# Decoder layer with selective scan, attention and top-2 experts: raw rows scattered, keys and values on ScalarE, routing scratch in PSUM

## The reference

```python
def mixer(x):                       # x: layernorm of the input
    h = layernorm(x) * ln_g + ln_b
    x_h, res = split(h @ W_in.T)    # 256 + 256 channels
    x_h = silu(causal_conv(x_h, 4 taps))
    dt, B, C = split(x_h @ W_x.T)   # 64, 16, 16
    dt = softplus(dt @ W_dt.T + b_dt)
    # scan over 256 positions, state 256 x 16:
    #   h = exp(dt * A) * h + dt * B * x_h ;  y = sum(h * C)
    y = (scan + x_h * D_param) * silu(res)
    return x + alpha * (y @ W_out.T)
x = x + mixer(layernorm(x))
x = x + cross_attention(layernorm(x), ctx, 16 heads, 64 keys, mask)
g = layernorm(x)
p = softmax(g @ Wg + bg)            # 8 experts
top 2 of p, weights softmax(p1, p2)
x = x + sum over the two of weight * (relu(g @ W1[e] + b1[e]) @ W2[e] + b2[e])
```

## Time and profile before

| what | value |
|---|---|
| median of 3 runs | 1040.76 us (1035.5 to 1041.91) |
| the profiled execution's own time | 1042.74 us |
| its span in the profile | 1040.9 us |
| busy: TensorE, VectorE, GpSimd, ScalarE | 787.0, 744.2, 704.4, 488.9 us |
| granted TensorE clock, mean | 0.865 of full |
| moved by DMA | 143.51 MB, 138 GB/s on average |
| longest scan-phase group on VectorE | scan L1332, 128 times, 292.6 us |

### The profile page before, as it was taken

The page is one execution under the profiler, slowest core; times in us unless marked ns, Lnnn a source line. Parts: engine busy times, 40 slices in busy tenths (PEclk is TensorE's granted clock), DMA queues, the critical chain, the costliest instruction groups (busy, mean ns, idle before and its releaser), DMA issues. The chain is left out here.

```text
span 1040.9 us, 12598 instructions
## 1 busy us (share of the span) xinstructions
PE 787.0 (76%) x3871; PEld 498.4 (48%) x3871; DVE 744.2 (71%) x1060; ACT 488.9 (47%) x1086; POOL 704.4 (68%) x501
## 2 busy tenths in 40 slices
PE   5667677797778778867877886774768998799592
PEld 1233343363344345334524542452446688798592
DVE  3279987989996897899789889958952625233172
ACT  3557456557475545746564674434213334232130
POOL 0159987978699779878977996787661445554252
PEclk9888788998899679878976997776688999999797
DMA  2324382282264228225522642385016446867872
GB/s 67 126 101 147 125 246 95 93 214 84 91 179 139 84 96 225 90 91 149 167 84 83 190 127 75 121 202 162 1 37 194 132 116 178 255 187 196 270 215 79
DMA packets 111076, 143.51 MB, mean 138 GB/s; under 512 B 18392, under 2 KB 83557, under 8 KB 111008
## 3 DMA queue, kind: packets, MB, share of 16 engines
q1 hardware_dynamic: 106016, 134.26, 43.9%
q0 software_dynamic: 4992, 8.45, 2.5%
HBM read 110.48 MB, written 34.01 MB: 139 GB/s over the span
## 5 line engine op out<-in xcount | busy, mean ns | idle before, releaser
L1185 POOL TENSOR_TENSOR prod<-hst,BC 128x1024 f32<-128x1024 f32 x128 | 303.9, 2374 | 121.6 <-DVE hst L1332 120.3
L1332 DVE TENSOR_TENSOR_SCAN hst<-dA,Rp 128x1024 f32<-128x1024 f32 x128 | 292.6, 2286 | 12.2 <-DVE Rp L1323 0.4
L993 ACT ACTIVATE dA<-dtm,Aneg 128x255 f32<-128x255 f32 x512 | 216.0, 495 | 146.4 <-DVE hst L1332 146.2
L571 PE MATMUL Y<-prod,ident 128*128 128x256 f32 x512 | 167.7, 461 | 65.0 <-POOL prod L1190 58.6
L1266 POOL DMA_INDIRECT y2d<-prod,BC x92 | 90.6, 984 | 136.6 <-DVE prod L1627 114.9
L571 PEld LDWEIGHTS Y<-prod,ident 128*128 128x128 f32 x512 | 108.5, 225 | 140.7 <-POOL prod L1190 93.8
L1190 POOL TENSOR_TENSOR prod<-prod 128x512 f32<-128x512 f32 x128 | 163.6, 1278 | 10.0
L1323 DVE TENSOR_TENSOR Rp<-BC,Rp 128x1024 f32<-128x1024 f32 x128 | 156.5, 1223 | 5.5 <-DMA BC<-bcd 1.5
L571 PE MATMUL Rp<-BC,prod 128*128 128x128 f32 x736 | 92.0, 279 | 8.2 <-DVE prod L1627 8.2
L571 PE MATMUL T<-Kbd,qT 64*128 64x512 f32 x128 | 62.5, 862 | 45.9 <-DVE mx L1376 45.9
L571 PEld LDWEIGHTS Rp<-BC,prod 128*128 128x128 f32 x736 | 90.5, 195 | 13.3 <-issue 10.8
(11 more groups left out here) (222 smaller groups left out, 1255.7 us busy)
## 6 DMA issues: line engine op xcount, KB each, us to landing
BC<-bcd SPq DMA_DIRECT2D x64, 1024.0 KB, 5.4
BC<-in_L_ffn_W SPq DMA_DIRECT2D x92, 256.0 KB
xsd<-blank SPq DMA_DIRECT2D x18, 1032.0 KB, 13.8
BC<-xsd SPq DMA_DIRECT2D x46, 129.0 KB
soft<-in_L_ffn_b SPq DMA_DIRECT2D x46, 64.0 KB
xin<-in_x SPq DMA_DIRECT2D x8, 256.0 KB, 4.1
x2d<-x2o SPq DMA_DIRECT2D x8, 256.0 KB
E<-x2d SPq DMA_DIRECT2D x1, 2048.0 KB
```

Source lines behind the costliest of these rows:

```text
L571: return pe.matmul(o, l, r_, start=start, stop=stop, **kw)
L993: m = A(dA[:, k % RING, i, 1:SEQ], dtm[:, r % 2, d, b * SEQ + 1:(b + 1) * SEQ], ACT.Exp, scale=Aneg[:, d, c * NC + i:c * NC + i + 1])
L1185: TT(prod[:, k % RING, :, :], hst[:, k % RING, :, :], BC[:, (k // 2) % BCR, 1, :, :], ALU.mult).then_inc(s_pd, 1)
L1332: v.tensor_tensor_scan(hst[:, k % RING].rearrange("p n s -> p (n s)"), dA[:, k % RING].rearrange("p n s -> p (n s)"), U.rearrange("p n s - ...
```

## The change

- The rows that are scattered are the raw ones: `x2o` itself gets 132 words a row, with the negated mean, the reciprocal spread, the token's index and its first expert behind the 128 channels. `rows_out` and `xs` go. The rows are normalised when a group is loaded: VectorE's new `tile_norm(j+2)` (two operations of 128 columns, and two of two elements for the index `back`) stands behind `tile_relu(j)`, and TensorE's `tile_in` waits for it.
- ScalarE copies keys and values (`copy_kv`) and makes `Kbd` in two halves of eight small copies with a scale (`key_blocks`). The contexts are loaded by one DMA of 512 KB and turned in round 0.
- The router's scaled logits are made by GpSimd with opposite sign (`scaled_logits`), VectorE takes their minimum (`least`), ScalarE makes four exponentials with their sums; no division follows in the round (one at the end, `softmax_gaps`). The picks and places pass through PSUM (`Picked`, `Placed`); the step's input product at steps 11 and 13 waits for that scratch. The counting matmuls read both choices, 10 matmuls instead of 5.
- Other slots: `mixer_out`, `logits`, `att_out` on VectorE at step 5 instead of 4; scores and maxima at 10 to 13; turned maxima at 14; `conv` half 1 at 6; turned scores behind the norm's matmuls; spreads at 6; keys and values stay at 6 with the centring after them.
- Scatters: two behind step 13, three behind 14 and 15 each.
- The residual comes in four loads of 512 KB at groups 21, 24, 27 and 30; the results' six loads stand one behind each of six groups' loads.

The diff, cut to what matters:

```diff
@@
-ROW = D + 1
+NM, RS, ID, E0 = D, D + 1, D + 2, D + 3
+ROW = D + 4
...
+        Picked = [t[:, 0:2 * NTT].rearrange("p (c t) -> p c t", c=2) for t in (scratch, sqt)]
...
             for j in range(PARTS[1].group, GROUPS):
                 load_group(j)
-                if j == PARTS[1].group + WR - 1:
+                n = j - PARTS[1].group - WR + 1
+                if n == 0:
                     scattered(PARTS[1].group)
-                    for i in range(early):
-                        load_results(i)
+                if 0 <= n < 2 * early:
+                    load_results(*divmod(n, 2))
...
-                pe.wait_ge(s_xr[j % XR], 16 * (j // XR + 1))
+                pe.wait_ge(s_nm, j + 1)
...
+            def key_blocks(r, half):
+
+                act.wait_ge(Ta.sem, Ta.at("KT", r))
+                if r and half == 0:
+                    act.wait_ge(Tp.sem, Tp.at("st11", r - 1))
+                for h in range(half * HP, (half + 1) * HP):
+                    m = A(Kbd[:, :, h, :], KT[:, :, :], ACT.Copy, scale=blk[:, h:h + 1])
+                m.then_inc(s_kb, 1)
...
-            def rows_out(r):
-
-                if r:
-                    act.wait_ge(s_xs, 16 * 2 * NTT * r)
                 for t in range(NTT):
-                    m = A(xs[:, t, :, 0:D], x2o[:, t, :].unsqueeze(1).to_broadcast([P, 2, D]), ACT.Identity, bias=nmr[:, t:t + 1],
-                          scale=spread[:, t:t + 1])
+                    at = r * NTT + t
+                    m = A(pr[:, t, :], nl[:, t, :], ACT.Exp, bias=lmin[:, t:t + 1], scale=-1.0, accum_out=lsum[:, at:at + 1])
...
-                if tail2 and k < 2 * NTT - 3:
-                    scatter(r - 3, k + 3)
...
+                        for n in ((0, 1), (2, 3, 4), (5, 6, 7))[k - STEPS + 3]:
+                            scatter(r - 2, n)
...
+                if r >= 2 and k in (11, 13):
+                    v.wait_ge(Fv.sem, Fv.at("hot" if k == 11 else "ch", r - 2))
...
+            def tile_norm(j):
+                n = j % XR
+                v.wait_ge(s_xr[n], 16 * (j // XR + 1))
+                if j >= 2:
+                    v.wait_ge(s_tt, j - 1)
+                for i in range(GT):
+                    m = v.tensor_scalar(xl[:, j % 2, i, :], xr[:, n, i, 0:D], xr[:, n, i, NM:NM + 1], xr[:, n, i, RS:RS + 1], ALU.add, ALU.mult)
+                m.then_inc(s_nm, 1)
...
             for j in range(GROUPS):
                 a, b = slots_of(j)
                 tile_relu(j)
+                if j + 2 < GROUPS:
+                    tile_norm(j + 2)
                 if j:
                     tile_out(j - 1)
```

More of the change, by code:

```diff
@@ L211, in decoder @@
         blank = sb("blank", [P, 2, ROW])
[L212 to L213 removed]
+        lg = sb("lg", [P, NTT, EXPERTS])
+        nl = sb("nl", [P, NTT, EXPERTS])
         sqs = sb("sqs", [P, D])
[L215 to L217 removed]
+        lmin = sb("lmin", [P, NTT])
         pr = sb("pr", [P, NTT, EXPERTS])
[L219 removed]
+        lsum = sb("lsum", [P, ROUNDS * NTT])
         top = sb("top", [P, NTT, 8])
@@ L236, in decoder @@
         pasts = xn2[:, 0:PARTS[0].groups * EXPERTS].rearrange("p (g e) -> p g e", e=EXPERTS)
-        expert = sb("expert", [P, PARTS[0].groups])
+        expert = sb("expert", [P, GROUPS])
         start = sb("start", [P, PARTS[0].groups])
@@ L332, in decoder @@
         s_ys = sem("s_ys")
-        s_acc = sem("s_acc")
+        s_acc = [sem(f"s_acc{i}") for i in range(FINAL)]
         s_y = [sem(f"s_y{i}") for i in range(YR)]
@@ L561, in _ @@
             for i in range(early, FINAL):
-                load_results(i)
+                for c in range(2):
+                    load_results(i, c)
             for i in range(early, FINAL):
@@ L1050, in slot @@
                 ln, nxt = ahead(r)
-                prev, tail, tail2 = behind(r)
+                prev, tail = behind(r)
+                if r == 0 and k in (6, 7):
+                    copy_contexts(k - 6)
                 if tail:
@@ L1160, in _ @@
                 if j == PARTS[1].group:
-                    act.wait_ge(Fv.sem, Fv.all(ROUNDS - 1))
-                    A(wt[:, 1, :], gaps[:, :], ACT.Exp).then_inc(s_wt, 1)
+                    act.wait_ge(s_wt, 2)
+                    A(wt[:, 1, :], wt[:, 1, :], ACT.Exp).then_inc(s_wt, 1)
         @block.gpsimd
@@ L1206, in row_ids, with picks, row_slots @@
                     pool.wait_ge(s_xs, 16 * 2 * NTT * r)
-                pool.tensor_copy(xs[:, :, :, D:ROW].bitcast(I32), ids[:, r, :, :].unsqueeze(3)).then_inc(s_id, 1)
+                pool.tensor_copy(x2o[:, :, ID], ids[:, r, :]).then_inc(Fg.sem, 1)
+            def picks(r):
+                pool.wait_ge(Fv.sem, Fv.at(f"i{NTT - 1}", r))
+                TT(gaps[:, r * NTT:(r + 1) * NTT], top[:, :, 1], top[:, :, 0], ALU.subtract).then_inc(Fg.sem, 1)
+                pool.tensor_copy(x2o[:, :, E0], topi[:, :, 0]).then_inc(Fg.sem, 1)
+            def row_slots(r):
+                pool.wait_ge(Fv.sem, Fv.at("sf", r))
+                if r:
+                    pool.wait_ge(s_xs, 16 * 2 * NTT * r)
+                pool.tensor_copy(slots[:, :, :], slotf[:, :, :]).then_inc(Fg.sem, 1)
             def scatter(r, n):
@@ L1448, in select @@
+                v.wait_ge(Fv.sem, Fv.at("pk", r))
                 every = iota[:, :].unsqueeze(1).unsqueeze(1).to_broadcast([P, 2, NTT, EXPERTS])
-                go(v.tensor_tensor(hot[:, :, :, :], picks, every, ALU.is_equal), "hot", r)
-                go(v.tensor_tensor(hits[:, NTT:2 * NTT, :], hot[:, 0], hot[:, 1], ALU.add), "hit", r)
+                v.tensor_tensor(hot[:, :, NTT:2 * NTT, :], Picked[part_of(r)].unsqueeze(3).to_broadcast([P, 2, NTT, EXPERTS]), every,
+                                ALU.is_equal).then_inc(Fv.sem, 1)
@@ L1460, in places @@
-                go(v.tensor_reduce(slotf[:, :, :], chosen[:, :, :, :], AX.X, ALU.add), "sf", r)
+                placed = Placed[part_of(r)]
+                from_ = first[:, part_of(r), :] if r in (0, SPLIT) else base[:, 1 - r % 2, :]
+                v.tensor_tensor(placed, got, from_.unsqueeze(1).to_broadcast([P, NTT + 1, EXPERTS]), ALU.add).then_inc(Fv.sem, 1)
+                v.wait_ge(Fv.sem, Fv.at("pos", r))
+                v.tensor_copy(base[:, r % 2, :], placed[:, NTT, :]).then_inc(Fv.sem, 1)
@@ L1597, in group_table @@
                 ov, pa, ps_ = over[:, :, 0:part.most], past[:, 0:n, :], pasts[:, 0:n, :]
-                then(v.tensor_tensor(tiles[:, :], pos[:, (part.last - 1) % 2, NTT, :], first[:, i, :], ALU.subtract))
+                then(v.tensor_tensor(tiles[:, :], base[:, (part.last - 1) % 2, :], first[:, i, :], ALU.subtract))
                 then(v.tensor_scalar(tiles[:, :], tiles[:, :], 1.0 / GROUP, None, ALU.mult))
@@ L1606, in group_table @@
                 then(v.tensor_tensor(ps_, pa, tiles[:, :].unsqueeze(1).to_broadcast(wide), ALU.mult))
-                then(v.tensor_reduce(expert[:, 0:n], pa, AX.X, ALU.add))
+                then(v.tensor_reduce(expert[:, at], pa, AX.X, ALU.add))
                 then(v.tensor_reduce(start[:, 0:n], ps_, AX.X, ALU.add))
```

381 lines of the change are left out of this document (213 added, 168 removed).

## The result

The changed kernel takes 995.94 us, the median of four runs (992.25 to 998.47), against 1041.03 us for the kernel before (1035.5 to 1041.91). The ratio is 0.9575, with a 95% interval of 0.953 to 0.962. The forecast of 985 was 11 us low; its range of 958 to 1018 holds the result. The profiled execution took 998.47 us with a span of 996.7, the one before 1042.74 and 1040.9.

What follows compares the result with a forecast made beforehand. VectorE was taken to set a round (busy 81.9 of 93.0 us), GpSimd next. 1042.7 less 37 (five full rounds), 3 (round without routing), 12 (last round) and 6 (groups) gave 984.7, so 985; range 958 to 1018.

Steps and rivals of the forecast that it cites:

- the walk: Computed times of one full round's points, counted from scan 13; claimed the next scan 13 ends at 85.6 us, against 93.0.
- 37 + 3 + 12 = 52 us: Rounds' gain: five full rounds 5 x 7.4 = 37, the round with attention but no routing 3, the last round 12.
- The PSUM scratch keeps VectorE free: Routing on VectorE: scratch in PSUM avoids exclusion by GpSimd's operations; chosen was to fall from 0.89 to 0.23 us.
- Eight are 1.4 us: ScalarE's key blocks: eight small copies take 1.4 us, at 0.17 for each further copy.
- 3 + 2.4 + 3 us: VectorE's idle places in a full round: before x1T at step 5, waiting for rstdt, and before positive at step 9.
- packing the scatters pays with 2.8 us: GpSimd's packed scatters move the gate from 34.6 to 37.4 us after scan 13, so VectorE's stall is only halved.
- Together −6: Groups: split loads giving 7 us and the normalisation costing 1 us make the stage 6 us shorter.
- I take 7: Groups: split loads of residual and results give 7 us, of at most 17 from holes of 7.2 and 9.9.
- Cost 1 us for the first group, up to 16 if 0.35 a group is uncovered: Normalisation on VectorE, some 0.9 us a group, claimed covered by tile_down beside the ReLU pair, so about 1 us.
- the first rival: ScalarE bounds steps 6 to 9; additions cost 10 instead of 5 us and VectorE waits; time 1016, chance 0.17.
- The fourth: Slower: TensorE stands 1.5 us in each of 46 groups for the normalisation, 69 us; time 1060, chance 0.04.
- TensorE's idle time before the row transposes over 20 us in all: Groups: one of the signs that would show the forecast wrong, the threshold being 20 us.

Runs made afterwards that it cites:

- e8: Changed kernel with picks and places in SBUF tiles of their own instead of PSUM; ratio 0.9673 to the kernel before.
- e6: Changed kernel with 14 further copies of key blocks a round on ScalarE, to a spare tile; ratio 0.9833 to the kernel before.
- e4: Changed kernel with all scatters one a step, in every round, instead of packed; ratio 0.9724 to the kernel before.
- e3: Changed kernel with the old loads: residual in one 2 MB load, six results' loads in a row; ratio 0.9573 to the kernel before.
- e5: Changed kernel without the two wide operations of tile_norm, so raw rows are turned; ratio 0.9443 to the kernel before.
- e2: Changed kernel with tile_norm(j+2) ahead of tile_relu(j) on VectorE instead of behind it; ratio 0.9497 to the kernel before.
- e9: e2 with scatters at 1 + 2 + 2 + 3 behind steps 12 to 15; ratio 0.9466 to the kernel before.
- e1: Changed kernel with the 16 scatters of rounds 6 and 7 one behind each slot instead of packed; ratio 0.9562 to the kernel before.

## Why the prediction was right, and where it was off

**The rounds: the walk right, the sum partly by luck.** Round length 85.3 against 85.6, and all points of the walk within 0.9 us. Forecast 37 + 3 + 12 = 52 us, measured 54.1, but term by term it is this: the five full rounds gave 32.2 and not 37, since the first two gained only 4.6 and 5.3 (4.9 us less than forecast together; no run shows why). The round without routing gave 4.4 and not 3. The last one gave 15.1 and not 12, the hand-over 4.1 and not 0, and round 0 lost 1.7 that no term has. The forecast's own waits for the last round, 2.4 and 3, add up to 5.4, of which its sum took 4.6.

**VectorE's share: right in kind, 1.9 us low.** 8.6 us less busy against a net 6.7; no routing operation is long any more. The reason given, scratch in PSUM, is shown for one operation: in e8 the copy of `base` becomes long in SBUF. "The PSUM scratch keeps VectorE free" is not shown for `chosen`, which stays at 214 ns in SBUF too.

**A term inside the walk was mis-sized.** "Eight are 1.4 us" is 2.43: 0.30 a copy and not 0.17. (The estimate of 0.29 that the forecast works out from the Trainium skill, "VectorE: DVE Perf Modes", the errata section, and sets aside is the one that the trace agrees with.) It added 2.1 us ahead of the absolute value, which nevertheless came only 0.9 late: `rstdt` was 0.4 early, and the pieces beside the blocks took 0.8 less than counted. So two errors cancelled; by the slope of e6, blocks at 1.4 us would leave a round some 2 us shorter, an estimate.

**The waits of VectorE: right in sum, not in place.** Forecast 3 + 2.4 + 3 us; the timeline has 1.19 + 1.03 before step 6, 1.69 at the norm, and 3.16 + 1.07 at step 9. Of the last, the walk had only the second, the absolute value; the first is for TensorE's state sums, behind which it is hidden. A further wait, 1.85 us for ScalarE's `rstd` at step 2, is new and not in the walk; GpSimd works without a pause from step 14's product to the gate, so this wait does not move the gate.

**Packing: the reason was incomplete.** The sentence "packing the scatters pays with 2.8 us" counts the delay of the gate, which came as computed. It leaves out what spreading would cost now that the rows lie in `x2o`: in e4 VectorE waits up to 7.5 us for them to land, and the three rounds are 4.4 to 6.2 us longer.

**The groups: wrong, and this is the whole miss.** "Together −6" was +9.9, 16 us off. Its first part, "I take 7" for the split loads, is 0 in e3 by ratio, with 4 us either way, and 3 to 6 us by single profiles from group 16 on. I had read the holes of the earlier trace rows as the price of large loads; they are, but the same bytes in pieces cost most of it again. Its second part, "Cost 1 us for the first group, up to 16 if 0.35 a group is uncovered", measured 10.5 us by the stage in e5. The cover named for it, `tile_down` over the ReLU pair and the two wide operations, holds in plain groups; 8.5 of the 10.5 us fall on groups 5 to 16. There the slots' scores and maxima stand between: VectorE comes to the ReLU late, and the transposes, which earlier needed only the rows, now wait for it (4.5 us in three waits in the changed kernel's first profile; the rest of the 8.5 is not traced to single waits). I priced a group without its slots. If the split gives 3 to 6 us, these two terms leave 2 to 5 of the 16 uncovered; the late results below, one wait of 9.5 to 11.0 us in the changed kernel against two or three of 5 to 7 in the kernel before, may be in it, which no run separates. Moving the normalisation ahead of the ReLU gives 8 us by ratio, 5 to 7 within its set (e2).

**The rivals.** ScalarE as the bound, the first rival, is right as a mechanism, together with GpSimd's side (e6: 4.1 us for 4.3; e9: 1.1), and was wrong only in what the additions cost in time. The fourth, the normalisation, had the right place, and a sixth of its price was measured: 10.5 us over 46 groups, 0.23 each and not 1.5. The way that the prediction adds to it, GpSimd kept from writing descriptors, doesn't show in GpSimd's records: the groups' scatters take 993 ns in the mean in the changed kernel, 993 without the normalisation (e5) and 984 in the kernel before. "TensorE's idle time before the row transposes over 20 us in all" was named as a sign against the forecast, and it came out at 24.8, of which 8.8 is one wait in the hole at group 17; but before it was 21.6 with the rows' load as the releaser, so the bar was set without looking at its starting value. The forecast's sign "no hole of 7 us at the residual's load" held: the transposes of groups 20 to 24 are 3.7 to 3.8 us apart.

**Left open: TensorE's results that arrive late.** In the changed kernel TensorE's records show `tile_up` at 837.90 and `tile_down` at 839.93, and the ReLUs that need the former start at 845.03 on ScalarE and 849.31 on VectorE (`remote`: nothing that the profile shows released it):

```profile
837.90 1.89 PE L589 MATMUL M<-prod,BC 128*128 128x256 f32 x8
839.93 2.02 PE L589 MATMUL Rp<-BC,prod 128*128 128x128 f32 x16
850.75 0.69 PE L916 MATMUL Y<-ident,prod 128*128 128x128 f32 x2 [8.79 <-DVE prod L1690]
```

```profile
849.31 0.88 DVE L1704 TENSOR_SCALAR prod<-M,soft 128x256 f32<-128x256 f32 x2 [9.52 <-remote]
```

The same waits, up to 7.2 us on VectorE, stand in the kernel before, around its scatters at 833 to 903. They were in every profile but those of e1 to e4, in whose set the kernel before was 6 to 10 us faster. They are beside scatters and group loads each time, packed or spread. Between 840 and 846 us SyncE too is slow in the changed kernel: it issues a group's loads 0.7 to 1.4 us apart, against 0.4 to 0.6 in e2, which has no hole (838 to 841 us). What holds the results back wasn't found.
